# A gated attention and feed-forward block: the attention probabilities turned in 32x32 blocks on VectorE and regrouped through memory instead of turned on TensorE, with a rearranged start and middle

## What is computed

```
xn      = layernorm(x)
queries = rope(xn @ Wq.T)                      # 32 heads of 128
keys    = rope(ctx @ Wk.T);  values = ctx @ Wv.T   # 8 heads
attn    = softmax(mask(queries @ keys.T * scale))
x       = x + tanh(g_xattn) * (attn @ values) @ Wd.T
x       = x + tanh(g_ffn) * ffn(layernorm(x))
```

## Time and profile before

| | us |
|---|---|
| three runs | 1571.01, 1572.49, 1574.35 |
| median | 1572.49 |
| the profiled execution, its own time | 1571.81 |
| its span, first to last instruction | 1570.0 |
| TensorE busy | 1483.4 |
| first score, start in the trace | 103.78 |
| last score, start in the trace | 1380.51 |

### The profile page before, as it was taken

How to read it: one execution, slowest core, us unless ns; L and a number is a source line. 1 busy time by engine, 2 the same in 40 slices (tenths; PEclk the granted TensorE clock), 3 DMA queues, 4 the chain that set the end, 5 groups by cost and what they waited for, 6 DMA issues and landing times.

```text
span 1570.0 us, 19226 instructions
## 1 busy us (share of the span) xinstructions
PE 1483.4 (94%) x7475; PEld 1218.4 (78%) x7488; DVE 988.2 (63%) x1536; ACT 537.5 (34%) x829; POOL 626.7 (40%) x403
## 2 busy tenths in 40 slices
PE   7869999999999999999999999999999999967996
PEld 7858888888888888877777888888888888854553
DVE  5837565656565656575655656565656565668995
ACT  4314141414141413244332414141313132317884
POOL 2525343434343333330434434333333333115996
PEclk9989999999999999999999999999999999998999
DMA  8633122322222222226151222221212221192553
GB/s 293 199 83 88 43 80 50 77 53 75 55 74 56 75 56 73 57 72 232 40 171 39 75 42 74 43 74 43 74 43 65 52 58 32 52 269 93 190 182 140
DMA packets 193786, 142.92 MB, mean 91 GB/s; under 512 B 147744, under 2 KB 162592, under 8 KB 193312
## 3 DMA queue, kind: packets, MB, share of 16 engines
q1 hardware_dynamic: 193264, 138.54, 31.0%
q0 software_dynamic: 432, 3.15, 1.0%
HBM read 124.88 MB, written 19.92 MB: 92 GB/s over the span
## 4 chain that ended last, share of the span: by engine, by line
PE 79%; DVE 7%; ACT 4%; DMA 3%; POOL 3%; SPq 2%; issue 2%; POOLq 0%; ACTq 0%
PE psum L502 16%; PE psum L504 16%; PE psum L503 16%; PE psum L556 7%; PE psum L591 7%; PE psum L593 7%; PE psum L592 7%; POOL go L1171 2%; PE psum L565 2%; DVE stat L1243 1%; DVE sc L1540 1%; ACT xg L1041 1%; SPq L321 1%; DMA wk_raw<-in_wk_t 1%; ACT xu L1042 1%
## 5 line engine op out<-in xcount | busy, mean ns | idle before, releaser
L502 PE MATMUL psum<-xt_hi,wq_hi 128*128 128x512 f32 x1024 | 405.9, 396 | 6.2 <-DVE rot L1295 5.2
L504 PE MATMUL psum<-xt_hi,wq_lo 128*128 128x512 f32 x1024 | 400.3, 391 | 0.0
L503 PE MATMUL psum<-xt_lo,wq_hi 128*128 128x512 f32 x1024 | 399.9, 391 | 0.0
L1103 POOL TENSOR_TENSOR rot<-rot 128x1024 f32<-128x1024 f32 x64 | 153.7, 2401 | 456.8 <-DVE rot L1303 455.1
L1351 DVE TENSOR_TENSOR acc<-psum,acc 128x512 f32<-128x512 f32 x256 | 176.0, 689 | 164.5 <-PE psum L593 162.5
L1075 POOL TENSOR_TENSOR wd_lo<-wd_raw,wd_hi 128x512 fp32r<-128x512 f32 x128 | 166.0, 1305 | 233.3 <-ACT wd_hi L848 233.3
L502 PEld LDWEIGHTS psum<-xt_hi,wq_hi 128*128 128x128 f32 x1024 | 193.3, 189 | 45.7 <-DVE rot L1295 5.6
L1199 DVE TENSOR_TENSOR vw_lo<-psum,vw_hi 64x512 fp32r<-64x512 f32 x256 | 176.3, 689 | 81.6 <-ACT vw_hi L884 75.9
L504 PEld LDWEIGHTS psum<-xt_hi,wq_lo 128*128 128x128 f32 x1024 | 192.9, 188 | 40.9
L884 ACT ACTIVATE vw_hi<-psum 64x512 fp32r<-64x512 f32 x256 | 151.7, 593 | 209.2 <-PE psum L504 206.0
L503 PEld LDWEIGHTS psum<-xt_lo,wq_hi 128*128 128x128 f32 x1024 | 193.2, 189 | 38.4
(11 more groups left out here) (128 smaller groups left out, 1982.0 us busy)
## 6 DMA issues: line engine op xcount, KB each, us to landing
wq_raw<-in_wq_t SPq DMA_DIRECT2D x128, 256.0 KB, 4.6
wd_raw<-in_wd_t SPq DMA_DIRECT2D x128, 256.0 KB, 3.1
acc<-in_x SPq DMA_DIRECT2D x16, 512.0 KB, 6.5
x_scratch<-acc SPq DMA_DIRECT2D x16, 512.0 KB, 6.8
xa<-x_scratch SPq DMA_DIRECT2D x16, 512.0 KB, 3.3
xb<-x_scratch SPq DMA_DIRECT2D x16, 512.0 KB, 4.3
xn<-in_x SPq DMA_DIRECT2D x10, 512.0 KB, 4.9
wk_raw<-in_wk_t SPq DMA_DIRECT2D x4, 1024.0 KB, 8.2
```

What stands on the lines that cost most here:

```text
L502: pe.matmul(dst, a_hi, b_hi, start=start, stop=False)
L503: pe.matmul(dst, a_hi, b_lo, start=False, stop=False)
L504: return pe.matmul(dst, a_lo, b_hi, start=False, stop=stop)
L1103: pool.tensor_tensor(rot[:, 0, :, :], rot[:, 0, :, :], rot[:, 1, :, :], ALU.add).then_inc(rope_done, 1)
```

## The change

Of the 32 units of a half, all but the last two are now `moved`: TensorE no longer turns their probabilities. After `softmax_b`, VectorE transposes `prob` in place in blocks of 32 by 32. SyncE, in `move_probs(unit - 1)` at the end of each unit's turn, waits for that, stores `prob` to a scratch tensor in HBM (one transfer), waits until the store has landed, waits for `pt_lo` of the unit before, and issues four reads of 32 partitions that bring the blocks back in their turned place, in `pt_raw` (512 runs of 128 bytes each). `copy_probs` and `lower_probs` read `pt_raw`. In each list they stand later in a slot than before: on ScalarE behind one or two `next_wq`. The subtraction of the next unit now waits for the store.

On TensorE the first four outputs of a group move back: output 0 stands behind `queries` part 4 instead of part 2, output 1 where 2 stood, and 2 with 3 in the next slot. `score` in a filled slot of kind 0 stands one part earlier. In the prologue the last key weights are loaded ahead of the first query weights, the second query weights are loaded ahead of the last key store instead of behind it, ScalarE turns the four rows tiles of the first slot over before it takes up the next query weights, and `normalise(0)` to `(3)` write to a part of the tile of `xt_lo` of their own, so that they don't wait for the transposes any longer. At the end of a half GpSimd makes the last low part of the output weights before it adds the rotated queries. In the second half the eight loads of x into `acc` are issued in two lots around the turn of unit 2, instead of in one behind unit 3.

```diff
+    p_dram = nc.dram_tensor("p_scratch", (2, 4, 32, BT, 4, 32), F32, kind="Internal").ap()
...
+        def moved(unit):
+            return unit % UNITS < UNITS - 2
...
             load_kv(6, whole, kv_in[6])
             store_kv(3)
+            load_kv(7, whole, kv_in[7])
             load_wq(0)
-            load_kv(7, whole, kv_in[7])
             store_kv(4)
...
             store_kv(6)
+            sp.wait_ge(kv_ps, KVB)
+            load_wq(1)
             store_kv(7)
...
+            def move_probs(unit):
+                n = moves(unit)
+                sp.wait_ge(turned_done, n)
+                sp.dma_start(p_dram[n % 2, :, :, :, :, :].rearrange("a q t c i -> (a q) (t c i)"),
+                             prob[:, :, :].rearrange("p s k -> p (s k)")).then_inc(p_out, 16)
+                sp.wait_ge(p_out, 16 * n)
+                if unit:
+                    sp.wait_ge(pt_lo_done, unit)
+                for c in range(4):
+                    sp.dma_start(pt_raw[32 * c:32 * c + 32, :, :, :],
+                                 p_dram[n % 2, :, :, :, c, :].rearrange("a q t i -> q t a i")).then_inc(pt_in[n % 2], 16)
...
+                    if u == 2 and half == 1:
+                        load_again(range(0, BT))
...
-                    if u == 3 and half == 1:
-                        for t in range(HTILES):
-                            sp.wait_ge(x1_store[t], 16)
-                            sp.wait_ge(part_done, TILES + t + 1)
-                            sp.dma_start(acc[:, t, :], x[HTILES + t, :, :]).then_inc(x_in[t], 16)
+                    if u >= 1 and moved(unit - 1):
+                        move_probs(unit - 1)
+                    if u == 2 and half == 1:
+                        load_again(range(BT, HTILES))
...
                 queries(unit, 0)
                 if kind == 0:
-                    if filled:
-                        turn_probs(unit - 2)
                     queries(unit, 1)
                     if filled:
                         values(gg - 1, 6)
                     queries(unit, 2)
                     if filled:
-                        outputs(gg - 1, 0)
+                        score(unit - 1)
                     else:
                         turn_rows(half, 4)
                     queries(unit, 3)
                     if filled:
-                        score(unit - 1)
                         values(gg - 1, 7)
                     else:
                         turn_rows(half, 5)
                     queries(unit, 4)
                     if filled:
-                        outputs(gg - 1, 1)
+                        outputs(gg - 1, 0)
...
                     if filled:
-                        outputs(gg - 1, 2)
+                        outputs(gg - 1, 1)
...
                 if kind == 1:
                     if filled:
-                        turn_probs(unit - 2)
+                        outputs(gg - 1, 2)
                         outputs(gg - 1, 3)
...
             def copy_probs(unit):
...
+                if moved(unit):
+                    act.wait_ge(pt_in[moves(unit) % 2], 64 * ((moves(unit) + 1) // 2))
...
                 if kind == 0 and filled:
-                    copy_probs(unit - 2)
                     copy_values(gg - 1, 6)
                     split_wd(VPG * gg - 1)
                     next_wq(unit, 0)
+                    copy_probs(unit - 2)
                     next_wq(unit, 1)
...
                     copy_rows(half, 4)
+                    copy_rows(half, 5)
+                    copy_rows(half, 6)
+                    copy_rows(half, 7)
                     next_wq(unit, 0)
-                    copy_rows(half, 5)
                     next_wq(unit, 1)
-                    copy_rows(half, 6)
...
+                split_wd((half + 1) * GROUPS * VPG - 1)
                 add_turned((half + 1) * UNITS - 1)
-                split_wd((half + 1) * GROUPS * VPG - 1)
...
             def normalise(t):
-                if t == 2 or t == 3:
-                    dve.wait_ge(xt_ps, t - 1)
...
-                if unit:
-                    dve.wait_ge(pt_ps, unit)
+                if unit and moved(unit - 1):
+                    dve.wait_ge(p_out, 16 * moves(unit - 1))
...
+                if moved(unit):
+                    blocks = prob[:, :, :].rearrange("p s (m k) -> p s m k", k=32)
+                    dve.wait_ge(p_done, unit + 1)
+                    dve.transpose(blocks, blocks).then_inc(turned_done, 1)
```

More of the change, by code:

```diff
@@ L148, in gated_block @@
             xt_hi = sb(s, "xt_hi", [EC, HTOK], F32R)
+            with ExitStack() as over:
+                xt_rows = sb(over, "xt_rows", [EC, HTOK], F32)
             xt_lo = sb(s, "xt_lo", [EC, HTOK], F32R)
@@ L161, in gated_block @@
             acc = sb(s, "acc", [HTILES, DIM], F32)
-            kv_b = sb(s, "kv_b", [2 * KVC], F32)
+            with ExitStack() as over:
+                kv_b = sb(over, "kv_b", [2 * KVC], F32)
+            pt_raw = sb(s, "pt_raw", [BT, 4, 32], F32)
         with ExitStack() as s:
@@ L279, in kv_bank, with moves, turns @@
             return bank(S_BANK + b % 2)
+        def moved(unit):
+            return unit % UNITS < UNITS - 2
+        def moves(unit):
+            return unit + 1 - 2 * (unit // UNITS)
+        def turns(unit):
+            return unit % UNITS - (UNITS - 2) + 1 + 2 * (unit // UNITS)
         def there(n):
@@ L400, in next_values, with load_again @@
                     load_v(gg)
+            def load_again(tiles):
+                for t in tiles:
+                    sp.wait_ge(x1_store[t], 16)
+                    sp.wait_ge(part_done, TILES + t + 1)
+                    sp.dma_start(acc[:, t, :], x[HTILES + t, :, :]).then_inc(x_in[t], 16)
             def store_rows(half, t):
@@ L520, in turn_rows @@
                 for ec in range(EC):
-                    ins = pe.transpose(turn_banks(half, t)[:, ec * P:(ec + 1) * P], rows_of(half, t)[:, ec * P:(ec + 1) * P], ident)
+                    ins = pe.transpose(turn_banks(half, t)[:, ec * P:(ec + 1) * P], rows_of(half, t)[:, ec, :], ident)
                 ins.then_inc(xt_ps, 1)
@@ L561, in turn_probs @@
                 pe.wait_ge(p_done, unit + 1)
-                if unit:
+                if turns(unit) > 1:
                     pe.wait_ge(pt_lo_done, unit)
@@ L1003, in _ @@
             copy_rows(0, 3)
+            for v in range(WDS):
+                split_wd(v)
             root(HTILES, slice(BT, HTILES))
@@ L1006, in _ @@
             act.activation(gates[:, :], gates[:, :], ACT.Tanh).then_inc(gate_done, 1)
-            for v in range(WDS):
-                split_wd(v)
             for half in range(HALVES):
@@ L1334, in lower_probs @@
                 dve.wait_ge(pt_hi_done, unit + 1)
-                lower(pt_lo[:, p, b, :], p_turned, pt_hi[:, p, b, :], pt_lo_done)
+                src = pt_raw[:, :, :, :].rearrange("p t a i -> p (t a i)") if moved(unit) else p_turned
+                lower(pt_lo[:, p, b, :], src, pt_hi[:, p, b, :], pt_lo_done)
             def lower_values(gg, i):
@@ L1382, in slot @@
                     if filled:
-                        lower_probs(unit - 2)
+                        add(gg - 1, 2)
                         add(gg - 1, 3)
@@ L1388, in slot @@
                     if filled:
+                        lower_probs(unit - 2)
                         add(gg - 1, 5)
@@ L1521, in _ @@
             reciprocal_root(2, slice(BT, HTILES), rstd1)
-            for t in range(BT, HTILES):
-                normalise(t)
+            normalise(4)
+            normalise(5)
             key_rows(7)
+            normalise(6)
+            normalise(7)
             dve.wait_ge(cst_in, 32)
```

57 lines of the change are left out of this document (31 added, 26 removed).

## The result

The changed kernel takes **1639.9 us** (median of four runs, 1638.2 to 1641.8) where the kernel before takes 1573.4 in the same session: 1.0425 times as long (95% interval 1.0406 to 1.0443), 66.5 us more. The forecast was 1606, 34 more. The sign and the place were right, the size was half of what came. The time lies outside the forecast's own range of 1585 to 1630, and within the wide one of 1563 to 1650.

The account below looks back on a forecast made before the run. TensorE, busy all the time in the slots, was taken to bound the kernel. Waits and slow clock +87, transposes -28, prologue -12, ends of halves -9.4, second half's start -3 give +34 on 1571.8: 1606 us, range 1585 to 1630.

Parts of the forecast that it names:

- The sign and the place: Slower by 34 us, with TensorE waiting for `pt_lo` at output 0 of 14 filled kind 0 slots; slower had 0.81.
- The cause: Filled kind 0 slots: ScalarE's copy stands behind a split whose query weights are now issued later, costing TensorE 4.6 us each.
- The chain, step by step: Filled kind 0 slot: transpose 0.69, store 2.3, reads' issue 2.55, weights 7.3, split, copy 0.60, low part 0.69 us.
- The low part: Filled kind 0 slot: VectorE's making of `pt_lo` after the copy, taken at 0.69 us.
- The clock: After a wait of about 4 us at output 0, TensorE's slow clock costs 1.6 us more, in 14 slots.
- forecast of 4.3: Growth of a group with a filled kind 0 slot: 4.6 us loss plus 1.6 for the clock, less the transposes saved.
- Elsewhere I cost these at nothing: Slots of kinds 1, 2 and 3, VectorE's added work and later outputs: the way is long enough, no cost.
- The second half's first group: Start of the second half: the 5.2 us wait for `rot` goes, score waits grow; net 3 us less.
- Prologue and halves: Prologue 12 us less, the ends of the halves 9.4 less, the second half's beginning 3 less.
- TensorE's 28 us: Transposes taken from TensorE for 60 of 64 units, 0.47 us each: 28 us less.
- That it would be faster: First rival: all links at low ends, loss 3.1 us per filled kind 0 slot, no slow clock; 1563 us, chance 0.15.
- Slow short reads: Second rival: 128-byte runs take 4.6 us instead of 2.3, query weights land 2 us later; 1635 us, chance 0.17.

Follow-up runs that it names:

- run 1: Changed kernel with ScalarE, in filled kind 0 slots, copying the returned probabilities before the first split of the query weights; 1576.7 us, ratio to before 1.0030.
- run 2: Changed kernel with SyncE issuing the next even unit's query weight loads between the probabilities' store and reads; 1562.2 us, ratio to before 0.9949.
- run 8: Changed kernel with copy first, weights between store and reads, score and output 0 one part later in filled kind 0 slots, two smaller moves; 1539.4 us, 0.9798.
- run 6: Changed kernel without store and reads, VectorE's transpose writing straight to `pt_raw`, orders kept; does not compute the attention; 1540.0 us, ratio to before 0.9801.
- run 4: Kernel before with only the prologue's and the half change's edits, probabilities still turned on TensorE; 1546.1 us, ratio to before 0.9840.
- run 11: run 8 with VectorE's statistics moved earlier in the second half's first two slots, and query weight loads in two pairs around the reads; 1528.8 us, 0.9726.
- run 7: Changed kernel with the four reads in runs of 2 KB instead of 128 bytes; does not compute the attention; 1627.4 us, ratio to before 1.0354.

## Why the prediction was right or wrong

**The cause: right, shown.** ScalarE waits for `wq_raw` right ahead of `pt_hi`, and TensorE 3.8 to 5.2 us for `pt_lo`, 14 times. Moving either one line in ScalarE's list (run 1) or the issue of the weights (run 2) takes most of the loss away. The kernel with the memory way in better orders (run 8, 1539.4) is as fast as the one without it in the old orders (run 6, 1540.0).

**The chain, step by step.** In the slot at 223.32 the transpose took 0.71 us (0.69 taken; the estimate of 1.24 from the Trainium skill, page "VectorE: DVE Perf Modes", section "The three transpose paths", does not fit, the measurement decides). The store took 2.27 (2.3), the issue of the reads 2.60 (2.55), the weights 7.40 from first issue to split (7.3), the copy 0.61. In the second half the weights took longer, 934.06 to 942.06, 8.0 us:

```profile
934.06 3.42 SPq L343 DMA_DIRECT2D wq_raw<-in_wq_t  x4
...
942.06 0.63 ACT L879 ACTIVATE wq_hi<-wq_raw 128x512 fp32r<-128x512 f32 x1 [7.96 <-DMA wq_raw<-in_wq_t]
```

**The low part: mis-sized.** I took 0.69 us from the earlier trace rows, where `pt_lo` reads PSUM. Now it reads `pt_raw` in SBUF, beside GpSimd's subtraction for the query weights, and takes 1.34; GpSimd's pair takes 2.96 where it took 2.54 in run 1. In run 1 the same instruction stands where GpSimd is idle and takes 0.68. The changed kernel's trace has the same split: of its 60 low parts from `pt_raw`, the 28 that meet no GpSimd instruction took 0.68 each, and of the 32 beside its subtractions 31 took 0.84 to 1.37. The loss of the slot is therefore 238.66 - (223.32 + 10.0) = 5.3 us, not 4.6, and about 6 in the second half.

**The clock: right mechanism, right size in the first half.** 1.6 us a slot was taken from one pair of rows; the slow stretches cost 1.7 in the inner groups of the first half and 2.0 in those of the second. With 5.3 and 1.7, less the 1.88 of the transposes, a group is 5.1 us longer, measured 5.3; with 6 and 2.0 it is 6.1, measured 6.2. Against the forecast of 4.3 the measured groups are 6 + 11 us over the twelve, half of what the forecast lacked: most of it by the low part (0.65 too small each time) and by the later weights of the second half (8.0 for 7.3).

**"Elsewhere I cost these at nothing": this step failed.** In the first group's kind 2 slot there is no filled work that gives time. SyncE issues the query weights 4.8 us behind the store, ScalarE waits 15.3 us for them with the exponential and `copy_values` behind, and TensorE waits 3.5 us for the values and then has 12 matmuls 0.43 us apart, some 2.5 us more. SyncE, ScalarE and TensorE:

```profile
101.92 0.33 SPq L440 DMA_DIRECT2D p_scratch<-prob  x1
103.97 2.68 SPq L446 DMA_DIRECT2D pt_raw<-p_scratch  x4
106.69 4.20 SPq L343 DMA_DIRECT2D wq_raw<-in_wq_t  x4
...
114.16 1.16 ACT L879 ACTIVATE wq_hi<-wq_raw 128x512 fp32r<-128x512 f32 x2 [15.31 <-DMA wq_raw<-in_wq_t]
...
120.79 0.77 PE L543 MATMUL psum<-wd_hi,v_t 128*128 128x512 f32 x1 [3.53 <-DVE vw_lo L1240]
```

The distance of scores 1 and 2, in which this lies, went from 15.9 to 21.9 us; in run 1, where only the copy moved, it was 20.6, in run 2, with the weights issued sooner, 16.4, and in run 6, without the memory way, 15.4. The whole first group lost 12.4 us where the forecast had 4.3.

**The second half's first group: mis-sized.** Net -3 was forecast for the beginning of the second half. The old wait of 5.2 for `rot` fell to 1.0, but three scores waited, 3.00, 3.06 and 4.13 us. The third had no counterpart in the sum: ScalarE waits 8.71 us for output weights with `pt_hi` behind them, the low part and the rotation behind that are late. The stretch is 7.9 us longer, where the forecast had one filled slot less transposes and this gain, about 1; 6 to 7 us.

```profile
828.00 2.02 PE L597 MATMUL psum<-kblk,rot 128*128 128x128 f32 x16 [3.06 <-POOL rot L1144]
...
847.17 3.07 PE L597 MATMUL psum<-kblk,rot 128*128 128x128 f32 x13 [4.13 <-POOL rot L1144]
...
832.55 0.63 ACT L884 ACTIVATE wd_hi<-wd_raw 128x512 fp32r<-128x512 f32 x1 [8.71 <-DMA wd_raw<-in_wd_t]
```

**Prologue and halves: right in sum, by luck in part.** 12 + 9.4 + 3 = 24.4 was the forecast, run 4 measured 26. Its parts were less exact: the first score came 9.2 us sooner in the changed kernel's profile and 10.9 in run 4's, the ends of the halves gave 2.6 and 4.1 there, less than the 9.4, and the second half's first group gave 7.2, more than the 3 (which allowed for VectorE's transposes; without them the forecast had 6.8). The eight transposes of the rows at full clock were put at 0.9 us; the trace has 1.03, and nothing hangs on it.

**TensorE's 28 us: right in size, but only 12 arrive.** Where nobody waits, the distance of two scores fell by 0.47 to 0.50 us for each set of transposes (22.67 to 22.20, 21.34 to 20.84), as taken. Groups of run 11 are 78.1 to 80.1 us where the sum of the work is 79.86 - 1.88 = 77.98. The rest goes to the waits of 0.2 to 1.5 us in ten of the 14 groups with a filled slot of kind 0, and to the matmuls behind them.

**The sum.** 1606 lacked 34 us. The inner groups hold 17 of them, the first group 8, the second half's first group 6 to 7, the prologue 3. Two steps failed: the price of the low part in the filled slot, 0.69 us where 1.34 came, and the unfilled slots that were costed at nothing, where 6 us came in the first group alone. **The rivals.** That it would be faster (0.15) needed all ends low; none was. Slow short reads (0.17) gave nearly the right time, 1635, for a reason that run 7 refutes. The wide range held because that rival had widened it, which is luck.

## What to carry to other kernels

When an instruction is given a later source, read the list ahead of it: what it stands behind may wait for a transfer that the change itself pushes back, and then the new path costs far more than its own length. The cure was in two orders, the copy ahead of the split, and the loads issued while the queue only waits for the store. And cost the unfilled slots at the start of a phase by themselves, since the steady slot says nothing on them.

## What the runs showed of the hardware

- VectorE's 128x512 f32 subtraction took 0.68 us from SBUF with GpSimd idle and 1.34 with GpSimd subtracting from SBUF; GpSimd's two went from 2.54 to 2.96. The same with a PSUM source took 0.69 beside GpSimd's addition, and 0.67 or 0.69 in the 16 places of the kernel before where it met GpSimd's subtractions.
- A wait of 4.3 us on TensorE left it at granted clock 0.60 and 0.75 in the next two windows, and the matmuls there lost 1.7 us; 3.6 us of unused matmuls in the wait made the kernel 31 us faster over 14 slots. A shorter wait, 3.20 us, was followed by a longer slow stretch.
- Four reads of 64 KB in runs of 128 bytes took 2.60 us to issue, in runs of 2 KB 1.72; the weights behind them took 7.0 us from issue to split instead of 7.4.
- VectorE's transpose of a 128x512 f32 tile in blocks of 32 by 32, in place, took 0.71 us, 60 times.
